# Perceiver layer on one core: score products in stretches of 2, 3 and 3 pairs, context remainders in four GpSimd pieces, values out of PSUM in one operation each

## What is computed

```python
q = split_heads(layernorm(x) @ q_w.T + q_b)
k = split_heads(context @ k_w.T + k_b)          # 16 heads of 32
v = split_heads(context @ v_w.T + v_b)
scores = q @ k.T / sqrt(32);  scores = where(mask > 0, -inf, scores)
x = x + softmax(scores) @ v
x = x + (n @ W_q.T) @ n.T @ n                   # n = layernorm(x), per batch
x = x + moe(layernorm(x))                       # 8 experts, top 2
```

## Time and profile before

| | |
|---|---|
| median of 3 runs | 1223.51 us (1223.32 to 1225.69) |
| the profiled execution, its own time | 1225.0 us |
| its span | 1223.2 us |
| PE busy | 1200.1 us (98%), 10197 matmuls |
| DVE, ACT, POOL busy | 842.1, 697.7, 213.6 us |
| mean granted TensorE clock | 0.998 |

### The profile page before, as it was taken

How to read it: one execution, slowest core, us unless ns; L and a number is a source line. 1 busy time by engine, 2 the same in 40 slices (tenths; PEclk the granted TensorE clock), 3 DMA queues, 4 the chain that set the end, 5 groups by cost and what they waited for, 6 DMA issues and landing times.

```text
span 1223.2 us, 25806 instructions
## 1 busy us (share of the span) xinstructions
PE 1200.1 (98%) x10197; PEld 1122.2 (92%) x10197; DVE 842.1 (69%) x2154; ACT 697.7 (57%) x1266; POOL 213.6 (17%) x239
## 2 busy tenths in 40 slices
PE   7999999999999999999999999999999999999997
PEld 6899999999999999999999999999879898899896
DVE  6656666566665666666566666777789887887876
ACT  6455545645654564564455456455656676687772
POOL 0004202410420251051023105101112000000012
PEclk9999999999999999999999999999999999999999
DMA  8102200220220031022003002200318777768663
GB/s 286 55 1 92 85 1 2 95 82 1 92 84 1 3 118 58 1 92 84 1 28 119 31 2 92 98 1 2 114 69 285 245 253 262 251 226 283 234 206 122
DMA packets 61059, 127.19 MB, mean 104 GB/s; under 512 B 3644, under 2 KB 21192, under 8 KB 60824
## 3 DMA queue, kind: packets, MB, share of 16 engines
q1 hardware_dynamic: 58776, 118.97, 28.6%
q0 software_dynamic: 2176, 6.72, 1.5%
HBM read 120.01 MB, written 14.32 MB: 110 GB/s over the span
## 4 chain that ended last, share of the span: by engine, by line
PE 90%; DVE 6%; ACT 2%; DMA 1%; issue 1%; SPq 0%; DVEq 0%
PE ptp L948 26%; PE work L948 22%; PE work L1335 8%; PE ptp_pv L1118 6%; PE work L986 6%; PE work L1337 3%; PE ptp L1358 2%; PE ptp L1361 2%; PE ptp L1359 2%; PE ptp L1360 2%; PE ptp L1362 2%; DVE kk_lo L1498 2%; ACT kk_hi L687 1%; PE work L1101 1%; DVE pt L1617 1%; PE work L955 1%
## 5 line engine op out<-in xcount | busy, mean ns | idle before, releaser
L948 PE MATMUL ptp<-vw_hi,cx_hi 128*128 128x256 f32 x832 | 242.2, 291 | 0.0
L948 PE MATMUL ptp<-vw_lo,cx_hi 128*128 128x256 f32 x832 | 235.7, 283 | 0.0
L948 PE MATMUL ptp<-vw_hi,cx_lo 128*128 128x256 f32 x832 | 235.7, 283 | 0.0
L948 PE MATMUL work<-cx_hi,kw_hi 128*128 128x400 f32 (+1 forms) x504 | 175.8, 349 | 1.3 <-DVE cx_lo L1519 1.3
L948 PE MATMUL work<-cx_hi,kw_lo 128*128 128x400 f32 (+1 forms) x504 | 173.6, 344 | 0.0
L948 PE MATMUL work<-cx_lo,kw_hi 128*128 128x400 f32 (+1 forms) x504 | 173.4, 344 | 0.0
L948 PEld LDWEIGHTS ptp<-vw_hi,cx_hi 128*128 128x128 f32 x832 | 159.5, 192 | 13.8 <-issue 12.7
L948 PEld LDWEIGHTS ptp<-vw_lo,cx_hi 128*128 128x128 f32 x832 | 159.6, 192 | 0.0
L948 PEld LDWEIGHTS ptp<-vw_hi,cx_lo 128*128 128x128 f32 x832 | 159.6, 192 | 0.0
L1498 DVE SCALAR_TENSOR_TENSOR kk_lo<-work,biasT,kk_hi 128x400 fp32r<-128x400 f32 (+1 forms) x128 | 79.5, 633 | 115.0 <-ACT kk_hi L687 114.9
L687 ACT ACTIVATE kk_hi<-work,biasT 128x400 fp32r<-128x400 f32 (+1 forms) x128 | 75.1, 595 | 127.2 <-PE work L948 124.5
(11 more groups left out here) (301 smaller groups left out, 2601.0 us busy)
## 6 DMA issues: line engine op xcount, KB each, us to landing
w1raw<-in_w SPq DMA_DIRECT2D x32, 1024.0 KB, 6.1
w2raw<-in_w SPq DMA_DIRECT2D x32, 1024.0 KB, 5.3
raw<-in_ctxT SPq DMA_DIRECT2D x31, 832.0 KB, 6.5
pr<-in_mask SPq DMA_DIRECT2D x8, 800.5 KB, 4.4
xrow<-x_rows SPq DMA_DIRECT2D x7, 256.0 KB, 5.3
y_rows<-y_out_rows POOLq DMA_DIRECT2D x7, 256.0 KB, 3.7
xs<-in_x SPq DMA_DIRECT2D x1, 1024.0 KB, 9.8
qwraw<-in_qwT SPq DMA_DIRECT2D x1, 1024.0 KB, 8.8
```

The costliest lines, as they stand in the source:

```text
L948: last = pe.matmul(dst, lhs(i, c), rhs(j, c), start=(c == 0 and (i, j) == (0, 0)), stop=(c == n - 1 and (i, j) == (1, 0)))
```

## The change

- Scores come in stretches of 2, 3 and 3 pairs instead of four of 2. The ring of score banks grows to six, `work[0..3]`, `ptp[2]` and `pv`. The first two turned blocks move from pair 3 to pair 2, which waits for v6's drain. v6 is made before the last score stretch.
- `query_blocks` moves from after the half's last score to after its fourth key step. `ctx_hi` of chunk 3 moves from after v6 to after the last exponential, and that exponential from before the first key step to behind it.
- `ctx_lo` becomes four operations of 128x416. Each part of a value step becomes one operation of 128x512.
- In the last half, the transposes `n` move up between v4 and v6, and q1 and q2 move in from the stage after: q0 and q1 before the first `w`, q2 before the second. Each `q` is four products of 384 columns; q0 was twelve of 128.

```diff
-        s = [[("s", 4 * h + 2 * i + rt, j) for j in (2 * u, 2 * u + 1) for rt in range(2)]
-             for i in range(2) for u in range(2)]
+        pairs = [[("s", 4 * h + 2 * i + rt, j) for rt in range(2)] for i in range(2) for j in range(NKC)]
+        s = [sum(pairs[low:high], []) for low, high in SCORE_WINDOWS]
...
-            steps += s[0] + v[0:1] + norms[0:1] + v[1:2] + s[1] + e[0:1] + v[2:3] + norms[1:2] + e[1:2] + v[3:4]
-            steps += norms[2:] + s[2] + v[4:6] + s[3] + t
-            steps += v[6:] + e[2:] + turned + w[:1] + queried + w[1:]
+            steps += s[0] + v[0:1] + norms[0:1] + v[1:2] + norms[1:2] + v[2:3] + s[1] + e[0:1] + v[3:4] + norms[2:] + e[1:2]
+            steps += v[4:5] + turned[:2] + v[5:6] + turned[2:] + v[6:] + s[2][:4] + t + s[2][4:] + e[2:]
+            steps += queried[:2] + w[:1] + queried[2:] + w[1:]
             continue
-        steps += s[0] + v[0:2] + s[1] + e[0:1] + v[2:3] + e[1:2] + v[3:4] + s[2] + v[4:6] + s[3]
-        steps += t + e[2:3] + v[6:] + e[3:]
+        steps += s[0] + v[0:3] + s[1] + e[0:1] + v[3:4] + e[1:2] + v[4:] + s[2] + t + e[2:3]
...
-            steps += k[:6]
+            steps += k[:1] + e[3:] + k[1:6]
...
-EARLY_Q = 1
+EARLY_Q = 3
+SCORE_WINDOWS = [(0, 2), (2, 5), (5, 2 * NKC)]
...
-PAIR_OF = [3, 3, 2, 0, 1, 2, 0, 1, 2, 1, 2, 0, 1, 2]
+PAIR_OF = [2, 2, 2, 0, 1, 2, 0, 1, 2, 1, 2, 0, 1, 2]
...
-    return [[vv[:, 2 * j:2 * j + n, :, rt, rt if hi else 1 - rt, :] for rt in range(2)] for hi in (True, False)]
+    parts = vv[:, 2 * j:2 * j + n].rearrange("p k g r a d -> p (k g) (r a) d")
+    return parts[:, :, 0:4:3, :], parts[:, :, 1:3, :]
...
-                pool.tensor_tensor(cx[1][:, :, sl], raw[:, k % 2], cx[0][:, :, sl].bitcast(F32),
-                                   ALU.subtract).then_inc(c_lo, 1)
+                for c in range(C):
+                    pool.tensor_tensor(cx[1][:, c, sl], raw[:, k % 2, c], cx[0][:, c, sl].bitcast(F32),
+                                       ALU.subtract).then_inc(c_lo if c == C - 1 else c_rows, 1)
...
-                    act.activation(dst[0], src[0], ACT.Copy)
-                    copy(dst[1], src[1], kv_hi)
+                    copy(dst, src, kv_hi)
...
-                pe.wait_ge(w_free, before_bank(b, last, both[1]))
+                pe.wait_ge(w_free, max(before_bank(b, last, step) for step in both))
+                if bank_of(last, both[0]) == 4:
+                    pe.wait_ge(pv_free, 4 * b + 2 * (a // 4) + 1)
...
-                    pe.wait_ge(pv_free, 4 * b + 2 * h + 1)
+                    pe.wait_ge(w_free, count(b, last, ("v", h, TPH - 1)))
...
+                if j % (2 * TPH) == 0:
+                    pe.wait_ge(w_free, before_pair(b, last, 2, ("w", g, 0)))
...
-                    dve.tensor_tensor(lo[0], src[0], hi[0].bitcast(F32), ALU.subtract)
-                    dve.tensor_tensor(lo[1], src[1], hi[1].bitcast(F32), ALU.subtract).then_inc(w_free, 1)
+                    dve.tensor_tensor(lo, src, hi.bitcast(F32), ALU.subtract).then_inc(w_free, 1)
...
-                    if step == ("s", 3, NKC - 1):
+                    if step == ("k", 1, 3):
                         query_blocks(b, 1)
-                    if step == ("s", 7, NKC - 1) and not last:
+                    if step == ("k", 0, 3):
                         query_blocks(b + 1, 0)
```

More of the change, by code:

```diff
@@ L162, in value_parts @@
 def value_parts(vv, j, n):
[L164 removed]
+    parts = vv[:, 2 * j:2 * j + n].rearrange("p k g r a d -> p (k g) (r a) d")
+    return parts[:, :, 0:4:3, :], parts[:, :, 1:3, :]
 def by_pair(bank, n):
[L169 removed]
+    return bank[:, 0:n * 2 * P].rearrange("p (n r d) -> p n r d", n=2 * n, r=2)
 def ring_banks(last):
@@ L176, in ring_banks @@
         if kind == "s":
-            banks.append(scored % 4)
+            banks.append(scored)
             scored, others, late = scored + 1, 0, False
-        elif kind == "w":
+            continue
+        if kind in "vkanq":
+            scored = 0
+        if kind == "w":
             others, late = 0, True
@@ L204, in before_bank @@
     other = max(m for m in range(len(RING[0])) if BANKS[0][m] == bank)
-    return NW * b + FIRST_K + max(ITEMS[0].index(RING[0][other]) + 1 - NW, bank - 3)
+    return NW * b + FIRST_K + max(ITEMS[0].index(RING[0][other]) + 1 - NW, min(bank - 3, 0))
 def before_pair(b, last, pair, weighed):
@@ L237, in layer @@
         sums = [ptp[2], pv]
+        ring = work + sums
         ident = sb(top, "ident", [P, P], F32)
@@ L777, in body @@
                         kv_item(b, last, step)
-                    if kind == "v" and a == 1 and j in LAST_READ and not last:
+                    if kind == "v" and a == 1 and j in LAST_READ and j < TPH - 1 and not last:
                         ctx_hi(b + 1, LAST_READ[j])
@@ L781, in body @@
                         exponentials(b, a)
+                    if step == ("e", 7, 0) and not last:
+                        ctx_hi(b + 1, LAST_READ[TPH - 1])
                     for j in turns(step):
@@ L826, in _ @@
             w1_part(0, 0, 0, True)
-            early_query(1)
+            early_query(C - 1)
             act.wait_ge(m_full, filled("b1"))
@@ L830, in _ @@
             root(3, range(EARLY, TT))
-            for m_ in range(2, C):
-                early_query(m_)
             turned(0, EARLY, yb[1])
@@ L985, in score_pair @@
                         rows = slice(2 * HD * rt, 2 * HD * (rt + 1))
-                        ins = pe.matmul(wide(work[bank_of(last, both[rt])], k), qbd[i][rows, cc, :],
+                        ins = pe.matmul(wide(ring[bank_of(last, both[rt])], k), qbd[i][rows, cc, :],
                                         kk[j][rows, cc, keys(k)], start=(i, j) == (0, 0), stop=(i, j) == (1, 0))
@@ L1009, in item @@
                 kind, a, k = step
-                bank = (ptp if spare(step) else work)[bank_of(last, step)]
+                bank = (ptp if spare(step) else ring)[bank_of(last, step)]
                 if kind == "s":
@@ L1030, in item @@
                     pe.wait_ge(ld2[1], 16)
-                    for t in range(EARLY):
-                        pe.wait_ge(w_free, count(b, last, ("n", 0, t)))
-                        tokens = slice(t * P, (t + 1) * P)
-                        ins = plain(bank[:, tokens], lambda c: wq2[:, c, k * P:(k + 1) * P], lambda c: hT[:, c, tokens])
-                    ins.then_inc(w_full, 1)
+                    pe.wait_ge(w_free, count(b, last, ("n", 0, EARLY - 1)))
+                    early_query(k, bank).then_inc(w_full, 1)
             READY = {(0, 0): ((kw0_hi, w_hi), (c0_hi, c_hi)), (0, 1): ((c0_lo, c_lo),), (1, 0): ((kw0_lo, w_lo),)}
@@ L1174, in _ @@
             pe.transpose(pv[:, 0:P], b1r[:], ident[:]).then_inc(m_full, 1)
-            for m_ in range(2, C):
-                early_query(m_, work[m_ - 1]).then_inc(m_full, 1)
             pe.wait_ge(ln2, TT)
@@ L1643, in body @@
                     kind, a, j = step
-                    for i in turns(step) if not (last and step == ("t", 2, 0)) else ():
+                    for i in turns(step):
                         pt_item(b, last, i)
@@ L1661, in body @@
                         item(b, last, step)
-                    if last and step == ("v", 1, TPH - 1):
-                        for i in turns(("t", 2, 0)):
-                            pt_item(b, last, i)
-                    if step == ("s", 3, NKC - 1):
+                    if step == ("k", 1, 3):
                         query_blocks(b, 1)
-                    if step == ("s", 7, NKC - 1) and not last:
+                    if step == ("k", 0, 3):
                         query_blocks(b + 1, 0)
```

14 lines of the change are left out of this document (8 added, 6 removed).

## The result

| | before | changed |
|---|---|---|
| median of 5 runs each | 1223.70 us (1223.32 to 1225.69) | 1230.33 us (1227.97 to 1231.65) |
| ratio, with its 95% interval | | 1.0046 (1.0031 to 1.0062) |
| the profiled execution, its own time | 1225.0 us | 1227.97 us |
| its span | 1223.2 us | 1225.2 us |
| PE, DVE, ACT, POOL busy | 1200.1, 842.1, 697.7, 213.6 us | 1195.6, 847.5, 691.4, 225.6 us |

A forecast was written before the change was run, and what follows sets the result against it. PE was taken as the bound, nine tenths of the chain of waits. The terms -5.85 + 0.7 + 1.15 - 0.7 + 1.4 gave -3.3 us, so 1220.2 us against a 1223.5 us median; 8-in-10 range 1217.4 to 1224.6 us.

The forecast's parts named there:

- Score stretches: PE in 15 halves: three score visits instead of four, each visit costing 0.39 us, so -5.85 us.
- The rival that a visit costs the same however cut: Score stretches on PE: the 0.39 us moves into the longer stretch, only losses stay, +2.9 us, 1226.4 us; chance 0.03.
- wait for v6's low part or the fifth bank: Rival: PE waits 0.1 us for v6's low part or the fifth key's bank in 15 halves, 1221.7 us; chance 0.21.
- Values in one operation: Value steps: one 128x512 copy instead of two of 128x256 is off PE's path, so nothing.
- GpSimd in four pieces: Context low part: a chunk takes 4.3 to 4.5 us instead of 3.8; nothing by itself.
- Query blocks: Seven halves with context: moved query blocks meet the last GpSimd piece, 0.1 us each, +0.7 us.
- the port: Rival: two or three GpSimd pieces each hold DVE for their length in seven halves, +3.7 us, 1227.2 us; chance 0.12.
- room of some 1.5 us per step: DVE in the key steps: 2.2 us apart on PE, needing 0.64, so the 2.2 us of query blocks fit.
- The last half: Until its second w ends: two more q, less 3.34 us of covered wait and one score visit, +1.15 us.
- The stage after: After the last w: the norm limits the last tokens' transposes, so only 0.68 us comes back, -0.7 us.
- The low clock: Stage after the last w: some 4.5 us of PE idle brings the 0.50 clock, +1.4 us.
- The case in which the clock does not fall: Stage after the last w: PE keeps its clock despite the idle time, 1218.1 us; chance 0.14.

The follow-up runs named there:

- e17: Changed kernel with each part of a value step again in two operations of 128x256, on ACT and DVE: 1232.23 us, ratio 1.0068 to the kernel before.
- e5: Changed kernel with the context's low part again one operation of 128x1664 instead of four of 128x416: 1231.27 us, ratio 1.0057 to the kernel before.
- e1: Changed kernel with GpSimd's four value-bias additions in batch 3 moved behind that batch's last sums: 1224.88 us, ratio 1.0003 to the kernel before.
- e6: Changed kernel with GpSimd's four value-bias additions left in place but each cut into four of 128x128: 1225.69 us, ratio 1.0013 to the kernel before.
- e2: Changed kernel with only the last batch's query blocks put back behind the half's last score: 1228.25 us, ratio 1.0035 to the kernel before.
- e11: Changed kernel with only the last batch's query blocks moved behind the seventh key's low part, between the two w: 1228.75 us, ratio 1.0035 to the kernel before.
- e15: Changed kernel with e1's late additions and the last batch in the old order, except v6 ahead of its last scores: 1219.30 us, ratio 0.9963 to the kernel before.
- e3: Changed kernel with q0 alone ahead of the last half's first w, the other q's in the stage after: 1230.55 us, ratio 1.0050 to the kernel before.
- e4: Changed kernel with q0 and q1 ahead of the last half's first w, q2 and q3 in the stage after: 1229.68 us, ratio 1.0045 to the kernel before.
- e9: Changed kernel with q0 ahead of the last half's first w, q1 ahead of the second, q2 and q3 after: 1228.47 us, ratio 1.0034 to the kernel before.
- e12: Changed kernel with e1, e9, e11 and the last half's first two turned blocks behind its last scores: 1218.51 us, ratio 0.9959 to the kernel before.

## Why the prediction was wrong

- **Score stretches**, -0.39 each: right to the hundredth in 13 halves. The two disturbed ones are 0.4 and 0.7 us ahead of the kernel before when their first w starts. The rival that a visit costs the same however cut is out; no wait for v6's low part or the fifth bank came.
- **Values in one operation**: nothing, right (e17).
- **GpSimd in four pieces**: 4.22 us a chunk where 4.3 to 4.5 were forecast, nothing on PE: right, and e5 shows that they also bring nothing.
- **Query blocks**: this is the step that failed. "Bounds per half: nothing, if the fourth piece and the casts do not meet, and 0.5 us" was worked out for a regular half and multiplied by seven. In six of the seven its times were right: counted from the half's first score, it had the pieces start at 31.5 us, DVE reach the query blocks at 34.7 and the pieces end at 35.9, and the trace has 31.4, 34.6 and 35.6. The casts did meet the last piece (1.85 to 1.87 us instead of 0.95) and PE paid nothing, where 0.1 was taken. In the seventh GpSimd's additions follow the chunk, which no row of the prediction shows, and that half paid 5.2 us against its neighbours: e1 gives them back, e6 most of them. The rival which the chances call the port, with 0.12, had DVE held for the length of each GpSimd piece. The traces show operations held until the GpSimd instruction beside them ends (1.20 to 1.27 us instead of 0.22 to 0.29), but not what holds them, and the rival put the loss on the context's pieces, the same in all halves, where it came from the additions in one.
- **Query blocks, last batch**: the same step's "room of some 1.5 us per step" was read in a half without the early tokens' norm. There the wait is 1.99 us, and with the saving taken off this half loses 1.7 us, 3.2 where the clock falls behind the wait. With them at the old place or between the two w it still loses 0.9 and 0.8 us (e2, e11), and e15 shows that v6 ahead of the last scores has a part in that, which the sum put at nothing from the rows of a regular half.
- **The last half**: +1.39, forecast +1.15. That q0 and q1 take away the whole 3.34 us (8.68 - 5.34, of it 1.93 idle) was right. The rest is the price of a q: the three took 5.36 and 2.78 us from start to start, 8.14 in all, where 2.58 each was forecast, 0.39 more; what stands ahead of them became 0.54 us shorter instead of 0.39. e3 and e4 showed what the step did not say: the first w's cover is time, not work, and one q has to stand ahead of the second w.
- **The stage after**: 0.68 us sooner, right. The low clock was mis-sized: 1.4 us taken, 2.0 measured (1.32 + 0.68). It lasted from about 889.4 to 896.2 us, and PE worked in it for 5.0 us; the stretch that gave the 1.4 was 3.4 us long (867.3 to 870.7). e4 and e9 have two q's there and the transposes equally early (8.92 us after the last w), no low clock, and 34.11 us, so against them the price is 2.4. The case in which the clock does not fall, 0.14 in the chances and worked out at 1218.1 us, is out: it was 0.50 behind the 4.32 us.

In the profiled span the forecast's -3.3 became +2.0: 5.2 and 1.7 us not foreseen, 0.9 us more in the last half and behind it, 0.7 less than forecast in the regular halves, and a start that was 1.6 us early by chance. Without that start it would be +3.7; the low clock that most traces have in the last batch makes it 5.2, the longer one in batch 3's half 5.9, and with the 1 us outside the span it is near the 6.6 between the medians.

**Open.** The 2, 3, 3 stretches were not tried alone on the kernel before. How the last batch's loss is shared between the query blocks, v6 and the last exponential was not separated. Why the last batch's first half is short in two traces of ten, with the clock at 1.00 behind the same wait, the runs do not tell.

## What to carry to other kernels

A step that moves in a loop moves in every round, also in the rounds that hold something extra (the branch for one batch, the last round's own steps): cost it in each of those, from their own rows, for every engine it will run beside. Small operations on DVE that take 0.22 to 0.29 us alone waited here until the GpSimd instruction beside them had ended, and took 1.20 to 1.27 us each beside additions of 1.3, so look for such long instructions on GpSimd beside them and move or cut them. Work moved ahead of a wait earns only if it is not needed as cover somewhere else: taken out of a later gap, it left 4.32 us of idle time here, and a granted clock of 0.50 for 6.8 us behind it.

## What the hardware showed unexpectedly

- Eight DVE operations of 32x128, 2.2 us alone, took 7.0 us beside a piece of 128x416 and four additions of 128x512 on GpSimd, and 4.0 with the same additions cut in sixteen. A held operation ended 0.08 to 0.15 us after the GpSimd instruction beside it (changed kernel and e6); one that had started 0.02 us ahead of the addition took its usual 0.22 us in both.
- After some 2 us of waiting (1.95 to 2.08, last batch's h = 0) the granted clock fell to 0.50 in eight traces and stayed at 1.00 in two; after waits of 3.2 to 3.5 us (batch 3) and some 4.3 us (the stage after) it fell in all nine traces that have them, and after 1.74 us in the stage after (e4, e9, e12) it did not. The price was 1.5 us in the last batch's first half (57.6 against 56.1) and 2.0 to 2.4 us in the stage after. The same schedule had the low clock for 3.4 us in some traces and for 6.8 in others: in batch 3's half that was 57.7 against 58.5 us.
